# Spreading B rows over the partitions: from an fp32 product to one product of a high and a low part

## The reference

```python
u, z = jnp.split(x @ in_w.T, 2, axis=-1)                 # 256 channels each
u = silu(causal conv of 4 taps over u + conv_b)
dbc = u @ xproj_w.T                                      # dt (64), B (16), C (16)
dt = softplus(dbc[..., :dt_rank] @ dt_w.T + dt_b)
Bm, Cm = dbc[..., dt_rank:dt_rank + d_state], dbc[..., dt_rank + d_state:]
dA  = jnp.exp(dt[..., None] * A)
dBu = (dt * u)[..., None] * Bm[:, :, None, :]
def step(h, inp):
    dA_t, dBu_t, C_t = inp
    h = dA_t * h + dBu_t
    return (h, jnp.einsum('bdn,bn->bd', h, C_t))
y = ys.swapaxes(0, 1) + u * D
return y * jax.nn.silu(z) @ out_w.T
```

## Time and profile before

| | us |
|---|---|
| median of 3 runs | 1466.38 (1465.43 to 1467.89) |
| span of the profiled execution | 1437.5 |
| median less that span: what lies around it | 28.9 |
| PE busy | 1295.8 (90%) |
| DVE busy | 1180.6 (82%) |
| POOL busy | 1063.1 (74%) |
| ACT busy | 954.9 (66%) |
| spreads L465, 224 records | 122.2 busy, 628 ns each |

### The profile page before, as it was taken

The page is one execution under the profiler, slowest core; times in us unless marked ns, Lnnn a source line. Parts: engine busy times, 40 slices in busy tenths (PEclk is TensorE's granted clock), DMA queues, the critical chain, the costliest instruction groups (busy, mean ns, idle before and its releaser), DMA issues.

```text
span 1437.5 us, 26311 instructions
## 1 busy us (share of the span) xinstructions
PE 1295.8 (90%) x9310; PEld 959.2 (67%) x9310; DVE 1180.6 (82%) x1941; ACT 954.9 (66%) x1762; POOL 1063.1 (74%) x668
## 2 busy tenths in 40 slices
PE   6799999999999999999999777998998999998995
PEld 3566666666666666666666655568997666666993
DVE  6889999999999999999999995433335788977776
ACT  6968977987887887797787784224555555453343
POOL 2989999999999999999999992531333466565573
PEclk9999999999999999999999998999999999999998
DMA  6123323322332322332332223231214200002233
GB/s 205 68 93 116 103 87 116 113 92 101 113 104 97 117 106 107 116 112 78 116 112 99 91 96 143 101 98 41 84 53 146 94 2 2 1 17 57 77 95 105
DMA packets 53873, 132.03 MB, mean 92 GB/s; under 512 B 8369, under 2 KB 33457, under 8 KB 44033
## 3 DMA queue, kind: packets, MB, share of 16 engines
q1 hardware_dynamic: 48976, 120.56, 24.2%
q0 software_dynamic: 4768, 9.81, 2.1%
HBM read 117.40 MB, written 18.56 MB: 95 GB/s over the span
## 4 chain that ended last, share of the span: by engine, by line
PE 39%; DVE 33%; issue 10%; ACT 8%; POOL 6%; DMA 2%; SPq 1%; DVEq 0%; POOLq 0%; ACTq 0%
DVE hh L900 16%; DVE hh L890 7%; DVE hh L871 4%; PE pq L396 3%; PE pa L498 3%; PE bank L1512 2%; PE bank L1522 2%; PE bank L1508 2%; PE py L519 2%; PE pr L2169 2%; PE bank L1428 2%; POOL hc L1049 2%; POOL ytoken L2029 2%; PE bank L1418 2%; PE bank L1419 1%
## 5 line engine op out<-in xcount | busy, mean ns | idle before, releaser
L1049 POOL TENSOR_TENSOR hc<-hh,cs 128x1024 f32<-128x1024 f32 x256 | 599.0, 2369 | 43.5 <-DVE hh L890 40.8
L519 PE MATMUL py<-ident,hc 128*128 128x128 f32 x2048 | 270.6, 276 | 27.7 <-ACT yt L730 22.7
L519 PEld LDWEIGHTS py<-ident,hc 128*128 128x128 f32 x2048 | 233.5, 142 | 89.1 <-issue 42.3
L900 DVE TENSOR_TENSOR_SCAN hh<-pa,st,hh 128x512 f32<-128x512 f32 x240 | 288.9, 1262 | 1.5 <-ACT pa L710 0.8
L710 ACT ACTIVATE pa<-dt,w 128x512 f32<-128x512 f32 x320 | 212.0, 683 | 56.3 <-DVE hh L900 51.7
L890 DVE TENSOR_TENSOR_SCAN hh<-da,st,pa 128x512 f32<-128x512 f32 x144 | 175.5, 1259 | 4.0 <-PE pa L498 2.7
L498 PEld LDWEIGHTS pa<-dg,dtut 64*128 64x128 f32 x1536 | 96.2, 189 | 85.2 <-issue 81.5
L498 PE MATMUL pa<-dg,dtut 64*128 64x128 f32 x1536 | 113.6, 286 | 40.4 <-DVE hh L900 36.2
L871 DVE TENSOR_TENSOR hh<-dtu,pb 128x1024 f32<-128x1024 f32 x112 | 134.3, 1199 | 1.3 <-PE pb L465 1.2
L465 PE MATMUL pb<-crow,sel 128*128 128x512 f32 x224 | 122.2, 628 | 9.6 <-DVE hh L871 9.5
L705 ACT ACTIVATE da<-dt,w 128x512 f32<-128x512 f32 x192 | 127.0, 712 | 0.0
(11 more groups left out here) (343 smaller groups left out, 2879.7 us busy)
## 6 DMA issues: line engine op xcount, KB each, us to landing
cs<-bcrows SPq DMA_DIRECT2D x64, 1024.0 KB, 4.7
bs<-bcrows SPq DMA_DIRECT2D x48, 256.0 KB, 3.6
xsorted<-in_pads SPq DMA_DIRECT2D x13, 387.0 KB, 5.4
rot<-in_rot SPq DMA_DIRECT2D x4, 1024.0 KB, 4.9
wx<-in_l_w SPq DMA_DIRECT2D x4, 1024.0 KB, 11.3
ysort<-ytoken SPq DMA_DIRECT2D x14, 256.0 KB, 4.8
wx<-in_l_w SPq DMA_DIRECT2D x1, 3072.0 KB, 11.3
wx<-in_l_w SPq DMA_DIRECT2D x1, 2304.0 KB, 17.8
```

Source lines behind the costliest of these rows:

```text
L519: i = pe.matmul(py[:, h * CH + kt * P:h * CH + (kt + 1) * P], hc[s % HCS][:, h, t], ident[:, :], is_transpose=True, start=n == 0 and kt == ...
L900: v.tensor_tensor_scan(hh[s % HHS][:, h, :], pa[i % SLOTS][:, :], hh[s % HHS][:, h, :], 0.0 if first else st[:, m % 2, n, h:h + 1], ALU.mu ...
L1049: g.tensor_tensor(hc[s % HCS][:, :, :], hh[s % HHS][:, :, :], cs[j % 2][:, s % CG, :].unsqueeze(1).broadcast_to([P, HF, CH]), ALU.mult).th ...
```

## The change

Every unit's B and C rows (32 rows on partitions 0 to 31, and a second copy of them on 32 to 63, which the weights of `x_project` make already) are kept once more in a type that PE multiplies in a single pass (`F32R`): the upper copy rounded to that type, the high part, and in the lower one what the rounding left, the low part. The low part is made by PE: `split` adds the rows and subtracts the high part in the bank `pq` (a 32-row fp32 product and a 32-row single-pass product), ACT then copies it out (`keep_low`). Each spread is now one single-pass product over these 64 rows, in which the constant `pick` has a one at the high and at the low row of state n, so that the two parts are added.

In the order of the work: on PE `x_project` moves from step n = 3 to n = 2 and `split` is added at n = 4; on ACT `keep_rows` moves from n = 4 to n = 3 and makes the high part as well, and `keep_low` is added at n = 5; `dt_project` now waits for the low part instead of for `crow`. Setup gains two small copies on ACT. (Line numbers of the changed kernel are some 6 to 25 higher: L396 becomes L402, L412 L418, L421 L433, L465 L479, L498 L512, L519 L533; on ACT L614 becomes L630, L710 L734, L705 L729.)

```diff
@@ -4,6 +4,7 @@
 import numpy as np

 F32, BF16, U32, I32 = mybir.dt.float32, mybir.dt.bfloat16, mybir.dt.uint32, mybir.dt.int32
+F32R = mybir.dt.float32r
 ALU, ACT, AX = mybir.AluOpType, mybir.ActivationFunctionType, mybir.AxisListType
 ds = bass.ds

@@ -214,6 +215,7 @@
             s_pin, s_dg = sem("inflow_by_tensor"), sem("b_diagonals_made")
             s_turned, s_turnk = sem("b_and_dtu_turned"), sem("b_and_dtu_kept")
             s_crow, s_cout = sem("bc_rows_kept"), sem("bc_rows_out")
+            s_high, s_split, s_low = sem("high_parts_of_bc_kept"), sem("low_parts_of_bc_made"), sem("low_parts_of_bc_kept")
             s_cin, s_bin = [sem(f"c_in{i}") for i in range(2)], [sem(f"b_in{i}") for i in range(2)]
             s_hc, s_st = sem("hc_made"), sem("state_kept")
             s_ysum = sem("y_summed")
@@ -229,6 +231,10 @@
                 keep = sb(k, "keep", [P, NCH + len(FACTORS) + 1])
                 sel = sb(k, "sel", [P, NS])
                 ident2 = sb(k, "ident2", [P, P])
+                minus = sb(k, "minus", [P, 2 * NS], F32R)
+                pick = sb(k, "pick", [P, NS], F32R)
+                parts = [sb(k, f"bc_parts{i}", [P, CH], F32R) for i in range(2)]
+                LOW, HIGH = slice(0, 2 * NS), slice(2 * NS, 4 * NS)
                 pre = sb(k, "pre", [P, 4, CH])
                 uz = [sb(k, f"uz{i}", [P, 4, CH]) for i in range(2)]
                 ab = sb(k, "ab", [P, HF, CH])
@@ -413,9 +419,15 @@
                                           start=h == 0, stop=h == HF - 1)
                         i.then_inc(s_xp, 1)

+                    def split(m):
+
+                        pe.wait_ge(s_high, m + 1)
+                        pe.matmul(pq[LOW, :], ident[HIGH, HIGH], crow[m % 2][HIGH, :], start=True, stop=False)
+                        pe.matmul(pq[LOW, :], minus[HIGH, :], parts[m % 2][HIGH, :], start=False, stop=True).then_inc(s_split, 1)
+
                     def dt_project(m, h):
                         if h == 0:
-                            pe.wait_ge(s_crow, m + 1)
+                            pe.wait_ge(s_low, m + 1)
                         elif m >= 1:
                             pe.wait_ge(s_ra, 2 * m + 1)
                         pe.matmul((pq if m >= 1 else py[:, h * CH:(h + 1) * CH])[:, :], wd[m % 2][P - RK:P, W_DT + h * P:W_DT + (h + 1) * P], crow[m % 2][P - RK:P, :],
@@ -443,8 +455,10 @@
                     def prep(m, n):

                         if m < UNITS:
-                            if n == 3:
+                            if n == 2:
                                 x_project(m)
+                            if n == 4:
+                                split(m)
                             if n in (5, 6):
                                 dt_project(m, n - 5)
                         if m >= 2 and m - 2 < UNITS - 1 and n in (8, 9):
@@ -462,7 +476,7 @@
                         if made(BY_V, s) >= 2:
                             pe.wait_ge(s_db, made(BY_V, s) - 1)
                         pe.wait_ge(s_turnk, min(turned_count(m, 2) + (1 if n - 2 > BT_AT else 0), turned_count(UNITS - 1, 2)))
-                        pe.matmul(pb[:, :], sel[:, n:n + 1].broadcast_to([P, P]), crow[m % 2][:, :], start=True, stop=True).then_inc(s_b, 1)
+                        pe.matmul(pb[:, :], pick[0:4 * NS, n:n + 1].broadcast_to([4 * NS, P]), parts[m % 2][0:4 * NS, :], start=True, stop=True).then_inc(s_b, 1)

                     def turn_b(m):

@@ -540,12 +554,14 @@
                     turn_x(1, s_nv, 4)
                     x_project(0)
                     z_half(0, 0)
+                    pe.wait_ge(s_wset, HF + 2)
+                    split(0)
                     pe.wait_ge(s_xv, 1)
                     dt_project(0, 0)
                     dt_project(0, 1)
                     z_half(0, 1)
                     turn_x(2, s_nv, 8)
-                    pe.wait_ge(s_crow, 1)
+                    pe.wait_ge(s_low, 1)
                     pe.wait_ge(s_w[1], 48)
                     pe.wait_ge(s_wneg, 3)
                     u_half(1, 0, (0, 1, 2, 3))
@@ -612,6 +628,12 @@
                             act.wait_ge(s_cout, 16 * (m - 1))
                             act.wait_ge(s_b, len(BY_V) * (m - 1))
                         act.activation(crow[m % 2][:, :], pq[:, :], ACT.Identity).then_inc(s_crow, 1)
+                        act.activation(parts[m % 2][HIGH, :], pq[HIGH, :], ACT.Identity).then_inc(s_high, 1)
+
+                    def keep_low(m):
+
+                        act.wait_ge(s_split, m + 1)
+                        act.activation(parts[m % 2][LOW, :], pq[LOW, :], ACT.Identity).then_inc(s_low, 1)

                     def first_abs(h):
                         act.wait_ge(s_din, h + 1)
@@ -657,8 +679,10 @@

                     def prep(m, n):
                         if m < UNITS:
-                            if n == 4:
+                            if n == 3:
                                 keep_rows(m)
+                            if n == 5:
+                                keep_low(m)
                             if n in (6, 7):
                                 relu_abs(m, n - 6)
                             if n == 7:
@@ -767,7 +791,9 @@
                     decay_rates(0)
                     act.wait_ge(s_const, 16)
                     diagonals(0)
-                    act.activation(ident2[:, :], ident[:, :], ACT.Identity, scale=2.0).then_inc(s_wset, 1)
+                    act.activation(ident2[:, :], ident[:, :], ACT.Identity, scale=2.0)
+                    act.activation(pick[:, :], sel[:, :], ACT.Identity)
+                    act.activation(minus[HIGH, :], ident[HIGH, HIGH], ACT.Identity, scale=-1.0).then_inc(s_wset, 1)
                     roots(range(4, TB), 2)
                     keep_pre(0, 0)
                     first_silu(0)
@@ -776,6 +802,7 @@
                     roots(range(TB, NT), 3)
                     act.activation(ab[:, 0, 0:1], eps[:, 0:1], ACT.Sigmoid)
                     keep_rows(0)
+                    keep_low(0)
                     first_abs(0)
                     first_abs(1)
                     sigmoid(0)
@@ -2770,7 +2797,7 @@
     k["pads"][:, D] = NT * P + np.arange(2 * SG * P)
     k["centre"] = np.eye(D, dtype=np.float32) - np.float32(1.0 / D)
     k["eye2"] = (np.arange(P)[:, None] % (P // 2) == np.arange(P // 2)).astype(np.float32)
-    k["sel"] = (np.arange(P)[:, None] == np.arange(NS)).astype(np.float32)
+    k["sel"] = ((np.arange(P)[:, None] % (2 * NS) == np.arange(NS)) & (np.arange(P)[:, None] < 4 * NS)).astype(np.float32)
     k["before"] = np.triu(np.ones((P, P), np.float32), 1).astype(mybir.dt.np(BF16))
     k["every"] = np.ones((P, P), mybir.dt.np(BF16))
     run = np.ones((NE, NT), np.float32)
```

## The result

The changed kernel takes 1531.72 us (median of 4 runs, 1529.56 to 1536.75), the kernel before 1467.14 beside it: a ratio of 1.0446, 95% interval 1.0425 to 1.0466, or +65 us. The forecast was +31, with a range up to 1520. The direction and the stall were right; the size was not.

A forecast was written before the change was run, and what follows sets the result against it. DVE was taken as the bound, busy 51.67 of 52.67 us a unit. Stalls less the gain gave +19.3, the start +1.7, the clock +10: together +31 us, so 1437.5 + 28.9 + 31 = 1497, range 1478 to 1520.

The forecast's parts named there:

- (e): PE's gap ahead of the inflow for step 11 grows to about 2.7 us, clock falls in half the units: +10.
- (a): Cheaper spread gives ACT its product of u 0.63 us earlier, ending DVE's softplus wait: -0.62 a unit.
- (b): x_project at n = 2 waits 2 us for silu, delaying step 5's spread and DVE: +1.4 a unit.
- (c): ACT's two extra copies delay step 9's exponentials, and dt_project waits for the low part: +0.6 a unit.
- (d): At the start, high copy, split and low copy precede the first dt_project: 2.3 us, of which 1.7 remains.
- clock falls in nearly every unit: Rival on PE's clock: +56 at most, about 1515 to 1522; chance 0.12.
- not a cheap product: Rival that the spread is not cheap: 1506 at 0.85 us a spread, about 1492 at 0.43; chance 0.10.
- Faster: Rival that PE's relief is worth its 0.62 and the x_project move is hidden: 1459; chance 0.06.
- same: Rival of no difference: stall only about 0.6, cancelled by (a), and the start hidden; chance 0.05.
- 28.9 around the span: Base of the forecast time: the profiled execution spans 1437.5 us and 28.9 lie around it.

The follow-up runs named there:

- e7: Changed kernel with two unread fp32 products ahead of x_project and two ahead of the inflow for step 11, filling both PE gaps: 1499.48 us, ratio 1.0235.
- before_again: The kernel before, unchanged, profiled once more: execution 1442.03 us, span 1440.0.
- e12: Changed kernel without split and low part (low part of B left out of the result), both PE gaps filled: 1482.34 us, ratio 1.0112.
- e13: Changed kernel with two unread fp32 products at n = 9, filling only PE's gap ahead of the inflow for step 11: 1507.49 us, ratio 1.0274.
- e10: Changed kernel without the split, the low part and their copies, gaps not filled: 1475.87 us beside 1439.55, ratio 1.0274.
- e3: Kernel before in its own order, with single-pass spreads over 64 rows, one more ACT copy, no split, low part left out: 1470.48 us, ratio 1.0023.
- e5: Changed kernel's arithmetic in the order of the kernel before, high copy at step 11, split at 14, low copy at 15: 1478.88 us, ratio 1.0089.
- e11: Changed kernel's arithmetic, x_project at n = 3, split at n = 9, high copy right behind the copy to crow at n = 4: 1472.94 us, ratio 1.004.

## Why the prediction was wrong, step by step

The step that failed is (e), the clock: +10 was forecast and the clock cost 31. A second and smaller part of the miss lies in the steps ahead of it, +21 forecast and 34 measured with the clock held. These are read from e7, where the clock fell at neither gap.

(a) "DVE's 0.62 goes": it did not. The wait for softplus is 5.1 us in e7 against 8.9 in the same stretch of before_again, so 0.27 a unit, less than half of what was forecast. The mis-sized term is the spread: 0.43 us of PE instead of 0.22. Of the two bounds given from above, the record of an fp32 product was the truth, and the bf16 row the wrong neighbour. By the Trainium skill, "FP8 and Floating Point Precision" (TensorE Precision Notes), the estimate was a quarter of 0.85; the rows show a half, and the measurement decides. The rest is beside the spread (PE of e7):

```profile
348.96 1.99 PE L402 MATMUL pq<-xn,w 128*128 128x512 f32 x4
350.88 0.50 PE L488 MATMUL pb<-bc_parts,pick 64*128 64x512 f32 x1
351.31 1.09 PE L542 MATMUL py<-ident,hc 128*128 128x128 f32 x8
```

The product ahead of the spread holds PE 1.92 instead of 1.83. The whole stretch up to the product that ACT waits for is 7.54 (347.87 to 355.41) instead of 7.81 (333.60 to 341.41), shorter by just those 0.27. About 5 us over the units.

(b) "PE stands for 2 us ... +1.4": PE waits 2.01 for silu, and DVE 1.49 for the spread at full clock. Right in place and size. The first unit was absorbed, as said: its stall is 1.23 in e7, in place of a wait of 1.17 right behind in before_again; in after it is 2.87, and the 2.09 of the earlier trace rows is gone. One thing was missed: the wait of 2.01 is itself a gap at which the clock falls. `x_project` took longer than 1.98 in 12 of 15 units, which is why DVE's stall is 3.13 in the unit shown and not 1.49.

(c) "+0.6 a unit": 0.70 or 0.71 ahead of step 9, where it was forecast and by ACT's exponentials. In total 15.6 against 6.6 in before_again, so 9.0 / 14 = 0.64. Right. PE's wait for the low part, 1.66, is there too. The rows of before_again (DVE, 36 to 872 us):

```profile
DVE dt L854 <- ACT pa L656: 8.9, 14, 0.8
DVE hh L900 <- ACT pa L710: 6.6, 10, 2.5
...
DVE hh L871 <- PE pb L465: 0.7, 1, 0.7
```

(d) "1.7 remains": the first scan starts at 42.28 instead of 39.45, 2.8. The bound of 2.3 was too low as well. The slack of about 0.6 ahead of POOL was there; it is the chain that was mis-sized: `dtu` starts at 38.53 instead of 35.20, 3.3 later where 2.3 was forecast. `dt_project` starts 2.5 later (28.21 instead of 25.71) and then takes 2.81 instead of 1.98, behind waits of PE of 0.93 and 0.77: the clock again. When the start as a whole begins differs from profile to profile by some 2 us, but from ACT's copy to `crow` to `dtu` it is 10.2 in before and in before_again, 13.8 in after and 10.8 in e12, which has the high copy and no split. So 0.6 of the delay is the high copy's, which POOL's slack hides, and 3.0 the split's and the low copy's.

At full clock DVE's waits make 21.9 (22.6 less the 0.7 of before_again) + 9.0 - 3.8 + 2.8 = 30 where the prediction had 19.3 + 1.7 = 21; e7 measured 34, with an interval of about 4 either way. Of the 9 us between the two sums (a) is 5 and (b) is 2.

(e) "I count half of the 14 units and half the price ... +10": the table gives 31. The gap became 3.04 us, not 2.7, and behind 12 of 14 the clock fell, not behind 7. The price was between the two that were weighed: a full fall cost 2.95, the whole of the earlier trace rows, but on average over the 12 it was about 2.0 and not 1.5. Together that is the 23 to 25 us of this gap. And the gap ahead of `x_project` was left out, though its 2 us stand in step (b); it is worth 6 to 8. The bound of 42 for this step would have given 1529, 2 us below the result; the range cut it off. Halving a count and a price was a guess: no row of before had a gap of this length that recurs.

The trace agrees here with the Trainium skill, "TensorE: Matmul & The Clock Gate" (HAM oscillation), that a wait which recurs in every pass of a loop can bring the lower clock in each of them; filling the gaps gave back 31 us in e7 and 25 in e13. The rival "clock falls in nearly every unit", +56 at most, was the right one in kind, had 0.12, and ended 10 us short of the time. The rival "not a cheap product", 1492 at 0.43, had the spread's price right and the clock wrong. Faster and same are excluded by the interval.

The "28.9 around the span" was wrong as told, since 2 us are; it did no harm, because the same 28 us stand in the comparison on both sides.

## What to carry to other kernels

If an in-order engine that is not the bound gets a cheaper instruction, what it saves becomes longer gaps, and here the longer gaps cost more (31 us) than the cheap product gave (some 25). Count the gaps first, at every place where the engine waits, and don't take a gap as harmless because it is short: gaps of 2.4 us were followed by slow products in half of the units or more, gaps of 3.0 in nearly all, and a fall cost about 2 us on average and 3 where it was full. When a step is moved up, look for its latest input, then for what is queued behind it, and do the same for every copy that feeds it: one copy moved in ACT's queue was worth 28 us, and moving the product back without its copies nothing. Put new work on PE where PE already waits, with its inputs made well ahead.

## What the runs showed of the hardware

- A single-pass product of 32-bit data with 512 columns holds PE 0.43 us from start to start, as long as one of the two records of the fp32 product, and not the quarter of the fp32 product that was estimated. That is the spread, 64 rows to 128; the one in `split`, 32 rows to 32, holds it 0.34 to 0.35.
- A short gap of PE can be followed by slow products, and its length alone does not decide it. Ahead of `x_project`: 12 of 15 gaps of 1.92 to 2.59 us in after, 7 of 15 such gaps in e13, where the other gap is filled, and 2 of 15 gaps of 1.71 to 2.48 in e10. Ahead of the inflow for step 11: 11 of 13 gaps of 2.83 to 3.05 in after, 6 of 13 gaps of 2.4 to 2.5 in e3 and in e5, 10 of 13 gaps of 2.20 to 2.43 in e10, 3 of 13 gaps of 0.9 to 1.2 in e11, and none of 13 gaps of 1.1 to 1.3 in e7.
- The same kernel took 1439.55 and 1466 to 1467 us in different batches. The profiles of changed kernels in the slower batches have one group of waits outside the Mamba block, 27.9 us in after, and those of the faster batch have none; the kernel before has no profile with them. Ratios within a batch were needed to compare anything.
